# A graph network's edge attention: the radial values as products over the whole array, with zeros beside the weights

## What is computed

```
rad = relu(edge_attr @ W1 + b1) @ W2          # W1: 16 x 64, W2: 64 x 64 (keys), 64 x 128 (values)
g = edge_sh @ Wang.T
k, v = (x_src * g @ Wlin) * rad               # one set of weights for keys, one for values
alpha = einsum('ehq,qk,ehk->eh', q[dst], Wdot, k)
attn = softmax of alpha over the edges of one target
out = segment_sum(attn * v, dst) @ Wout
```

## Time and profile before

| | |
|---|---|
| median of 3 runs | 4736.28 us (4735.1 to 4736.41) |
| the profiled execution, its span | 4794.0 us |
| TensorE busy, share of the span | 4150.5 us, 87% |
| VectorE busy | 3250.4 us, 68% |
| GpSimd busy | 2169.6 us, 45% |
| ScalarE busy | 1982.2 us, 41% |

### The profile page before, as it was taken

How to read it: one execution, slowest core, us unless ns; L and a number is a source line. 1 busy time by engine, 2 the same in 40 slices (tenths; PEclk the granted TensorE clock), 3 DMA queues, 4 the chain that set the end, 5 groups by cost and what they waited for, 6 DMA issues and landing times. The chain is left out here.

```text
span 4794.0 us, 72650 instructions
## 1 busy us (share of the span) xinstructions
PE 4150.5 (87%) x26457; PEld 3130.6 (65%) x26457; DVE 3250.4 (68%) x3936; ACT 1982.2 (41%) x2675; POOL 2169.6 (45%) x2000
## 2 busy tenths in 40 slices
PE   3666556999999999996499999999999999999952
PEld 3555545888888888885266666666666666666642
DVE  6887865555455545444378888888888888888845
ACT  4555544555555555442133333333333333333313
POOL 4555530000000000002677777777777777777544
PEclk8777778999999999997699999999999999999975
DMA  7999997878788887541577777777777777777636
GB/s 98 86 88 89 84 65 244 253 244 263 241 255 250 247 259 242 177 135 43 133 192 205 207 206 205 205 204 201 203 206 203 204 205 206 201 203 205 183 120 65
DMA packets 1013902, 877.73 MB, mean 183 GB/s; under 512 B 705567, under 2 KB 811435, under 8 KB 1013413
## 3 DMA queue, kind: packets, MB, share of 16 engines
q1 hardware_dynamic: 951605, 742.04, 63.8%
q0 software_dynamic: 61936, 130.95, 12.9%
HBM read 594.87 MB, written 277.52 MB: 182 GB/s over the span
## 5 line engine op out<-in xcount | busy, mean ns | idle before, releaser
L2178 POOL DMA_INDIRECT e_x_rows<-x_table,src_s x1616 | 1643.2, 1017 | 555.3 <-issue 450.4
L1183 PE MATMUL acc<-t_wide,scaled 128*128 128x512 f32 (+1 forms) x6370 | 1418.4, 383 | 24.3 <-DVE t_wide L1275 24.3
L1183 PEld LDWEIGHTS acc<-t_wide,scaled 128*128 128x128 f32 x6370 | 1157.0, 188 | 268.4 <-issue 24.7
L1275 DVE CAST t_wide<-t_ring 128x1792 fp32r<-128x1792 uint8 x490 | 536.0, 1094 | 691.0 <-PE acc L1183 691.0
L1218 ACT CAST t_wide<-t_ring 128x1280 fp32r<-128x1280 uint8 (+1 forms) x490 | 646.7, 1320 | 645.3 <-PE acc L1183 645.3
L1649 POOL MEMSET l_wdot<- 64x64 f32 x1 | 0.1, 148 | 1462.0 <-POOLq L1381 1462.0
L578 PE MATMUL lists_rows_ps<-lists_hot_lo,lists_hot_hi 128*128 128x196 fp8e4 x3200 | 400.1, 296 | 254.4 <-ACT lists_staged L357 182.2
L578 PEld LDWEIGHTS lists_rows_ps<-lists_hot_lo,lists_hot_hi 128*128 128x128 fp8e4 x3200 | 355.5, 115 | 296.6 <-ACT lists_staged L357 193.4
L2357 ACT COPY e_out_rows<-e_turn_ps 128x1024 f32<-128x1024 f32 x202 | 204.7, 1013 | 681.8 <-PE e_turn_ps L2218 681.8
L357 ACT CAST lists_staged<-lists_rows_ps 128x784 uint8<-128x784 f32 x400 | 308.8, 819 | 297.8 <-DMA adjacency_bytes<-lists_staged 191.6
L2218 PE MATMUL e_turn_ps<-e_weighted,e_spot 128*128 128x128 f32 x3232 | 414.4, 281 | 10.9 <-DVE e_weighted L2449 10.8
(11 more groups left out here) (262 smaller groups left out, 5064.3 us busy)
## 6 DMA issues: line engine op xcount, KB each, us to landing
sums_table<-e_out_rows SPq DMA_DIRECT2D x202, 576.0 KB
t_ring<-adjacency_bytes SPq DMA_DIRECT2D x245, 400.0 KB, 3.6
t_ring<-adjacency_bytes SPq DMA_DIRECT2D x245, 384.0 KB, 4.0
q_first<-hop_zeros_q SPq DMA_DIRECT2D x101, 512.0 KB, 4.8
e_sh<-parts_sh SPq DMA_DIRECT2D x404, 128.0 KB
e_ea<-parts_ea SPq DMA_DIRECT2D x404, 128.0 KB
e_q_rows<-q_first SPq DMA_DIRECT2D x404, 128.0 KB
e_same<-same_row SPq DMA_DIRECT2D x404, 128.0 KB
```

Of the source, the lines that this page charges most:

```text
L1183: mm = nc.tensor.matmul(acc[c][:, 0:n], U[p][:, b, :], wide[m % WIDE_RING][:, lo:lo + n], start=(b == 0 and p == 0), stop=(b == NB - 1 and ...
L1275: nc.vector.tensor_copy(wide[m % WIDE_RING][:, 0:SHARE], ring[m % RING][:, 0:SHARE]).then_inc(wide_dve, 1)
L2178: nc.gpsimd.indirect_dma_start(x_rows[i % XR][:, g * GT + t, :], None, x1_table, bass.IndirectOffsetOnAxis(ap=src_ix[:, at:at + 1], axis=0 ...
```

## The change

The radial values of a tile of both groups come from one product: the hidden layers of both groups are the stationary operand, on all 128 rows, and `w2v` gets 256 columns, W2v in rows 0 to 63 of the first 128 columns and in rows 64 to 127 of the other 128, zeros elsewhere. There are four products in a round, each of 128 by 256. In the ring buffer the results of a tile stand side by side, group 0 and then group 1, so VectorE reads them by (group, tile) with steps. `w2v` is cleared by GpSimd, and two DMAs fill its halves after that.

```diff
-        w2v = sb("w2v", [2 * HID, D])
+        w2v = sb("w2v", [2 * HID, 2, D])
...
+        values_clear = sem("values_clear")
...
-        n_w = 16 * 12
+        n_w = 16 * 13
...
-            for dst, name in ((w2k, "W2k"), (w2v, "W2v")):
-                sp.dma_start(dst[:], a[name].unsqueeze(0).to_broadcast([2, HID, dst.shape[1]])).then_inc(w_in, 16)
+            sp.dma_start(w2k[:], a["W2k"].unsqueeze(0).to_broadcast([2, HID, DQ])).then_inc(w_in, 16)
+            sp.wait_ge(values_clear, 1)
+            for g in range(2):
+                sp.dma_start(w2v[g * HID:(g + 1) * HID, g, :], a["W2v"]).then_inc(w_in, 16)
...
             nc.gpsimd.memset(w_all_f[:], 0.0).then_inc(w_clear, 1)
+            nc.gpsimd.memset(w2v[:], 0.0).then_inc(values_clear, 1)
...
             def radial_values(i, j):
                 bank = ring_bank(5 * i + 3)
+                by_tile = bank[:].rearrange("e a (b c) -> e (a b) c", c=2 * D)
                 for t in range(GT):
                     at = slice(t * P, (t + 1) * P)
-                    for g in range(2):
-                        rows = slice(g * 64, (g + 1) * 64)
-                        mm = nc.tensor.matmul(bank[:, g, at], hid_v[rows, j % VR, at], w2v[rows, :],
-                                              start=True, stop=True)
+                    mm = nc.tensor.matmul(by_tile[:, t, :], hid_v[:, j % VR, at], w2v[:], start=True, stop=True)
                 mm.then_inc(p_rv, 1)
...
-                nc.vector.tensor_tensor(weighted[j % 2][:].rearrange("e k d -> e (k d)"),
-                                        ring_ps[(5 * i + 3) % 2][:].rearrange("e g c -> e (g c)"),
-                                        lw[:].rearrange("e k c -> e (k c)"), ALU.mult).then_inc(v_weighted, 1)
+                by_tile = ring_ps[(5 * i + 3) % 2][:].rearrange("e a (b g d) -> e g (a b) d", g=2, d=D)
+                nc.vector.tensor_tensor(weighted[j % 2][:].rearrange("e (g t) d -> e g t d", g=2), by_tile,
+                                        lw[:].rearrange("e (g t h) c -> e g t (h c)", g=2, t=GT),
+                                        ALU.mult).then_inc(v_weighted, 1)
```

## The result

The changed kernel takes 4793.52 us (median of 4 runs, 4791.33 to 4796.96) against 4735.69 for the kernel before, measured with it: a ratio of 1.0125, with a 95% interval of 1.0113 to 1.0137. It is slower by 58 us; 60 had been forecast.

What follows compares the result with a forecast made beforehand. The prediction took TensorE to bound the kernel: 56.3 us for 194 rounds, 3.0 and 0.3 for the last ones and 0.4 for setup make 60 us, added to the 4736.28 median: 4796 us, range 4783 to 4822.

Steps and rivals of the forecast that it cites:

- TensorE as the bound: Full rounds of the attention stage: TensorE, busy 2099 of 2133 us, sets a round's length; no new wait on VectorE.
- The price of a full pass: Radial products on TensorE: a full pass of 256 columns costs 0.218 us, between 0.2135 and 0.227, priced by columns.
- rival 1: Radial products: a pass costs by its count, not its columns; -17 us, so 4719, up to no change; chance 4%.
- Rival 2: Attention rounds: GpSimd's gathers, at 11.3 us or more per round, hide the added 0.29; 4740 us; chance 2%.
- Rival 3: VectorE's product with the weights: the interleaved read makes it dearer by over a microsecond; 20 us more, 4816; chance 4%.
- Rival 4: Radial products: each product of 256 columns is cut in two; +0.03 us per round, 4803; chance 3%.
- The stretch: From transposes L2291 to L2256 in a round: 2.87 us becomes 3.16, +0.29 per round, 56.3 us over 194 rounds.
- The gap behind L2278: TensorE waits behind the half passes for ScalarE's copy of the turned rows; some 0.16 us of added work costs nothing.
- The last rounds: Last 8 rounds, without L2300: VectorE's product with the weights starts 0.43 us late; 3.0 us for seven rounds.
- The setup: Ahead of the first rounds: GpSimd clears more, 0.30 us, SyncE issues one more DMA, 0.52; overlapping, 0.4 for both.
- L2302's two starts: Two passes right behind the radial products: starts 0.22 us apart instead of 0.32, their load of weights being covered.
- L2452's idle time: VectorE's product with the weights waits for TensorE, some 0.2 us idle before it, which it had not before.

Runs made afterwards that it cites:

- e1: Changed kernel with each product of 256 columns cut into two of 128, still on all rows; 4809.28 us against 4736.58 for the kernel before, ratio 1.0149.
- e2: Changed kernel with the 16 half passes of the kernel before, but its cleared weights, second DMA and a stepped read kept; 4734.15 us against 4736.58, ratio 0.9995.
- e4: Kernel before with the first tile's two products done twice, 20 half passes a round; 4752.38 us, ratio 1.0037 to the kernel before.
- the new order: Kernels with two value products, transposes, six value products, L2300, then radial values; half passes took 4733.81 us against 4735.05 for the kernel before on a third chip.
- e3: Kernel before with the two loops of the radial values exchanged, all tiles of group 0 and then of group 1; 4817.97 us, ratio 1.0172.
- e12: Kernel before with its half passes in the new order, third try, on a third chip; 4733.81 us against 4735.05 for the kernel before, ratio 0.9996.
- e8: Changed kernel once more, unaltered, on a chip where the kernel before took 5761.19 us; 5683.77 us, ratio 0.9867.
- e10: Changed kernel, with its full passes, in the new order, run again on another chip; 5692.09 us against 5729.1 for the kernel before.
- e9: Kernel before, with its half passes, in the new order, run again on another chip; 5782.04 us against 5729.1 for the kernel before.

## Why the prediction was right

- **TensorE as the bound.** It still has one named wait in full rounds, for the softmax's copy, and none on VectorE. Right.
- **The price of a full pass**, 0.218 taken, measured 0.216. The doubling by columns holds, and rival 1 (a price by count) fell with e1: 16 passes of 128 columns take 1.70 us to L2304 and 8 of 256 1.55, with L2302's part shifted as below. The Trainium skill, "TensorE: Matmul & The Clock Gate", section "Back-to-back issue gap", gives a sustained 81 ns per matmul at 128 columns and 131 ns at 512, a growth by 1.6. The 4-byte stream here does not follow that: it grows by 1.9 from 128 columns (0.112 us, e1) to 256 alone (0.216 us).
- **The other rivals.** Rival 2, the gathers of GpSimd, did not hide anything: from 2500 to 4500 us TensorE has no wait for them, and they wait 126.0 us for TensorE, against 104.3 before. Rival 3 is answered under e2. Rival 4, products cut in two, is out by the row of L2281: 8 passes of 256 columns.
- **The stretch**: 3.16 forecast, 3.17 measured; +0.29 per round forecast, +0.30 measured, 194 x 0.30 = 58.
- **The gap behind L2278**, 0.16 from the rows, 0.17 by e4. This was the term most easily missed: without it, and without the load and the switch back to full rows behind L2278, the step would have been the 0.64 of the new order and the forecast 4736 + 194 x 0.64 + 3.7 = 4864 us.
- **The last rounds**: 0.43 forecast, 0.41 measured. The prediction gave no size for TensorE's wait ahead of L2218: it fell from 1.54 to 1.32, as the products end 0.63 later in the round and L2222 starts only 0.41 later.
- **The setup**, 0.4, has not shown. The clearing took 0.30, but the first transposes start 19.2 us after the stage's first memset, and did so 20.1 us after it before. Between two executions this is no measurement.
- **L2302's two starts** were to stand 0.22 apart. They stand 0.42 apart, the first only 0.03 behind the last start of L2281; the sum of both steps, 0.45, is what 0.22 + 0.22 gives. So the record of a start need not be where the array begins. By the record the copy L2382 ends 0.34 ahead of L2302, where the prediction had some 0.5.
- **L2452's idle time**, 0.2 forecast, 0.19 measured.

The terms of the sum thus add to 58 + 3 = 61 us in the trace, and 58 in the medians; the 3 us between lie within the interval of the ratio (54 to 65 us).

## What to carry to other kernels

Two products on different halves of the array's rows, next to each other in the queue, cost one: padding them with zeros to one full product halves the number of instructions and doubles the streaming time, so first look whether pairs already start together. What such an edit costs in a kernel is its price less the gap at its place: lay out the starts on the bounding engine, and ask what the next instruction waits for. And an order that closes a gap in three rounds of four must be read in the fourth as well.

## What was not expected

**Partners need not be neighbours.** In e3 all passes of one half stand ahead of all of the other, and three pass times still overlapped, 0.34 us: the first pass of the second half started beside one that stood four places ahead of it in the queue. What limits the reach was not measured.

**A record of a start can lead the array.** In the changed kernel the first pass of L2302 is recorded at 3509.18, while the last pass of L2281 before it, which streams for 0.22 us, starts at about 3509.15.

**Chips on which the attention stage takes other time.** On two of the four chips that e1 to e12 ran on, the kernel before took 5729 and 5761 us. No trace of it was kept there, but one of the changed kernel (e8): its hop stage takes 1429 us, as on the first chip, while from the first start of the radial values to the last it is 3028 us instead of 2248, which are 781 of the 894 us that this execution is longer. Whether that belongs to the chip or to the hour is open, since each chip was used once. The waits of ScalarE and VectorE in that trace, 2500 to 4500 us:

```profile
ACT e_out_rows L2359 <- remote: 960.6, 128, 8.6
```
```profile
DVE e_x_gv L2426 <- remote: 464.9, 125, 5.5
```

and one of these rounds:

```profile
3999.20 0.50 PE L2321 MATMUL e_ring_ps<-e_sh,e_stack 64*128 64x512 f32 x2
3999.62 0.65 PE L2248 MATMUL e_score_ps<-e_prod,e_head_sum 128*64 128x256 f32 x4
...
4003.97 1.01 ACT L2359 COPY e_out_rows<-e_turn_ps 128x1024 f32<-128x1024 f32 x1 [8.41 <-remote]
4004.02 1.22 DVE L2426 TENSOR_TENSOR e_x_gv<-e_ring_ps,e_x_t 128x1024 f32<-128x1024 f32 x1 [4.57 <-remote]
...
4005.24 0.66 PE L2238 MATMUL e_turn_ps<-ident,e_weight 128*128 128x128 f32 x2 [4.96 <-ACT e_out_rows L2359]
...
4006.54 3.62 PE L2272 MATMUL e_ring_ps<-e_wlin_v,e_x_gv 128*128 128x128 f32 x16
```

Both engines wait for matmuls (L2222 and L2321) that are recorded as long over, and go on within 0.05 us of each other, more than 4 us late. TensorE then stands 4.96 us for ScalarE's copy, and pays again behind it: the 16 passes of L2272 last 3.62 us instead of 1.95, at a granted clock of 0.50 from 4006.5 to 4010, the 1.2 GHz level, where it was 1.00 ahead of the wait (3995 to 4000). From 2418 to 5400 us the granted clock is 0.92 in this trace, against 1.00 from 2418 to 4551 in that of the first chip. In the changed kernel's trace from the first chip, whose rounds are those above, L2426 waits for L2321 alone, 191.4 us in 194 rounds, some 1 us each. What holds the matmuls or their signals back, once per round, the traces do not say, and no run was made for it. It turns the order of the kernels round: full passes beat half passes there by 1.3 to 1.6% (e8 against before; e10 5692 against e9 5782), and two half-row products more, which cost 0.22 us of TensorE's time per round, cost 58 to 69 us. That fits a bound which counts instructions more than columns, but this is a guess: a wait and the half-speed stretch behind it fall on other products in each order, and that was not separated. For the kernel as it runs on the other chips, the change is a loss.
